# A recommender tower on one core: every burst's pair weights loaded as two tiles of 64 columns instead of one of 128

## What is computed

```python
e = jnp.stack([tbl_0[ids[:, 0]], ..., tbl_39[ids[:, 39]]], axis=1)      # 2048 x 40 x 32
vi = e[:, _I_IDX, :]; vj = e[:, _J_IDX, :]                              # 780 pairs
z = jnp.einsum('bke,kef,bkf->bk', vi, W, vj)
h = jnp.concatenate([z, dense_ctx], axis=1)
h = jnp.maximum(h @ W_top1 + b_top1, 0.0)                               # 796 -> 512
h = jnp.maximum(h @ W_top2 + b_top2, 0.0)                               # 512 -> 256
y = h @ W_top3                                                          # 256 -> 1
```

## Time and profile before

| | us |
|---|---|
| median of 3 runs | 719.52 |
| lowest and highest | 717.11, 720.22 |
| the profiled execution | 717.67 |
| span of its trace | 715.9 |
| PE busy in it | 661.3 |
| DVE busy | 548.0 |
| POOL busy | 441.1 |
| ACT busy | 67.3 |

### The profile page before, as it was taken

The page is one execution under the profiler, slowest core; times in us unless marked ns, Lnnn a source line. Parts: engine busy times, 40 slices in busy tenths (PEclk is TensorE's granted clock), DMA queues, the critical chain, the costliest instruction groups (busy, mean ns, idle before and its releaser), DMA issues.

```text
span 715.9 us, 13728 instructions
## 1 busy us (share of the span) xinstructions
PE 661.3 (92%) x5912; PEld 189.6 (26%) x5912; DVE 548.0 (77%) x518; ACT 67.3 (9%) x104; POOL 441.1 (62%) x452
## 2 busy tenths in 40 slices
PE   0769999997999999999889999999999999999998
PEld 0322232322222223232222222222222222222222
DVE  3858999987976679798777677979997677879900
ACT  4100000000001010001000110010001110010002
POOL 6777777777777777777777777777777730000000
PEclk9988999998999999999989999999999999999999
DMA  8761111033021111101322111011202200000000
GB/s 278 280 160 30 29 28 28 15 88 85 14 46 29 28 31 28 28 15 29 103 53 48 29 31 28 13 29 21 51 14 47 43 15 11 16 16 16 1 4 1
DMA packets 25124, 33.22 MB, mean 46 GB/s; under 512 B 10276, under 2 KB 18212, under 8 KB 24296
## 3 DMA queue, kind: packets, MB, share of 16 engines
q1 hardware_dynamic: 9720, 22.94, 10.6%
q0 software_dynamic: 14336, 7.37, 6.9%
q10 hardware_dynamic: 1008, 2.04, 0.8%
HBM read 21.77 MB, written 0.06 MB: 30 GB/s over the span
## 4 chain that ended last, share of the span: by engine, by line
PE 63%; DVE 12%; POOL 11%; issue 9%; DMA 3%; ACT 1%; DVEq 0%
PE t_ps L543 19%; PE z_ps L564 18%; POOL rows L364 11%; PE x_ps L583 11%; DVE prod L480 9%; PE t_ps L583 3%; PE x_ps L596 3%; DVE one_hot L458 3%; PE x_ps L505 3%; PE t_ps L551 2%; PE x_ps L521 2%; DMA hot_sb<-hot_ids 2%; PE x_ps L607 1%; PE t_ps L596 1%; ACT e_t L401 1%
## 5 line engine op out<-in xcount | busy, mean ns | idle before, releaser
L480 DVE TENSOR_TENSOR prod<-t_ps,e_t 128x1024 f32<-128x1024 f32 x400 | 467.9, 1218 | 99.6 <-PE t_ps L543 60.2
L364 POOL DMA_INDIRECT rows<-tbl,idx x448 | 440.9, 984 | 140.2 <-issue 135.9
L543 PE MATMUL t_ps<-e_t,w_sb 32*128 32x512 f32 x1440 | 223.4, 648 | 14.6 <-DVE prod L480 14.6
L564 PE MATMUL z_ps<-prod,select 128*32 128x512 f32 x1600 | 218.5, 604 | 2.0 <-DVE prod L480 1.3
L543 PEld LDWEIGHTS t_ps<-e_t,w_sb 32*128 32x128 f32 x1440 | 67.5, 185 | 169.9 <-DVE prod L480 89.1
L505 PE MATMUL x_ps<-one_hot,tables 128*32 128x512 bf16 x1272 | 85.8, 387 | 28.1 <-DVE one_hot L458 24.9
L458 DVE TENSOR_SCALAR one_hot<-hot_sb,row_number 128x2048 bf16<-128x2048 f16 (+1 forms) x112 | 79.7, 748 | 20.5 <-DMA hot_sb<-hot_ids 17.8
L583 PE MATMUL x_ps<-z_sb,w_sb 128*32 128x512 f32 x672 | 84.5, 601 | 0.0
L564 PEld LDWEIGHTS z_ps<-prod,select 128*32 128x32 f32 x1600 | 45.6, 110 | 102.9 <-issue 52.0
L505 PEld LDWEIGHTS x_ps<-one_hot,tables 128*32 128x32 bf16 x1272 | 29.5, 97 | 98.7 <-issue 41.5
L401 ACT COPY e_t<-x_ps 128x512 f32<-128x512 f32 x40 | 23.5, 587 | 270.5 <-PE x_ps L505 154.0
(11 more groups left out here) (18 smaller groups left out, 46.4 us busy)
## 6 DMA issues: line engine op xcount, KB each, us to landing
rows<-tbl,idx POOLq DMA_INDIRECT x448, 2.4
hot_sb<-hot_ids SPq DMA_DIRECT2D x4, 1536.0 KB, 7.3
e_t<-e_t SPq DMA_DIRECT2D x80, 64.0 KB
e_t<-e_t SPq DMA_DIRECT2D x40, 128.0 KB
w_sb<-w_lay SPq DMA_DIRECT2D x1, 1792.0 KB
z_sb<-hot_tables ACTq DMA_DIRECT2D x2, 640.0 KB, 6.3
w_sb<-w_lay SPq DMA_DIRECT2D x1, 1152.0 KB, 12.9
w_sb<-w_lay SPq DMA_DIRECT2D x1, 896.0 KB, 10.4
```

What stands on the lines that cost most here:

```text
L364: pool.indirect_dma_start(out=rows[:, slot, t, E * f:E * f + E], out_offset=None, in_=tables[PER * c + f], in_offset=bass.IndirectOffsetOn ...
L480: nc.vector.tensor_tensor(prod[:, u % PROD_SLOTS, :, :], t_ps[:, at:at + 2, :], by, ALU.mult).then_inc(mult_done, 1)
L543: mm = nc.tensor.matmul(t_ps[:, at + r % 2, :], w_sb[part, b, :], e_t[part, e_slot(k, g), :], start=True, stop=True)
L564: mm = nc.tensor.matmul(z_ps[E * q:E * q + E, :], select[:, E - PER - PER * s:2 * E - PER - PER * s], prod[:, u % PROD_SLOTS, q % 2, :], s ...
```

## The change

The two branches of `gen` become one: the bursts with g < c are written with the same inner loop over `side` as those inside a group. Each of their four matmuls with weights of 32x128 becomes two with weights of 32x64, which write partitions 0 to 63 and 64 to 127 of the same bank. Source rows, weights in SBUF, results, waits and semaphore counts stay as they were; the increment stays on the last matmul of r = 1 and of r = 3.

```diff
                     if g < c:
-                        mm = nc.tensor.matmul(t_ps[:, at + r % 2, :], w_sb[part, b, :], e_t[part, e_slot(k, g), :],
-                                              start=True, stop=True)
+                        near = far = e_slot(k, g)
                     else:
                         near, far = e_slot(k, c + r // 2), fold_slot(k, c + r // 2)
-                        for side in range(2):
-
-                            source = far if (r, side) in ((1, 0), (3, 1)) else near
-                            cols = slice(P // 2 * side, P // 2 * side + P // 2)
-                            mm = nc.tensor.matmul(t_ps[cols, at + r % 2, :], w_sb[part, b, cols], e_t[part, source, :],
-                                                  start=True, stop=True)
+                    for side in range(2):
+
+                        source = far if (r, side) in ((1, 0), (3, 1)) else near
+                        cols = slice(P // 2 * side, P // 2 * side + P // 2)
+                        mm = nc.tensor.matmul(t_ps[cols, at + r % 2, :], w_sb[part, b, cols], e_t[part, source, :],
+                                              start=True, stop=True)
```

## The result

| | before | after |
|---|---|---|
| median | 719.06 us (717.11 to 720.22, 5 runs) | 713.54 us (713.47 to 715.32, 5 runs) |
| ratio | | 0.9933, 95% interval 0.9912 to 0.9953 |
| profiled execution, its span | 717.67, 715.9 us | 713.47, 711.6 us |

The kernel got faster, by 4.8 us (0.67%) in this comparison. A closer one, with 8 runs of the changed kernel and 25 of the kernel before, gave less: 0.9966, interval 0.9954 to 0.9978, which is 2.4 us. The forecast was 2.6. On one other chip the same change cost 2.7 to 3.0%. Its ratio, put on the 719.5 us that the forecast started from, gives 714.7, and that of the closer one 717.1; both are inside. The forecast's own ratio, 0.9964, lies in the interval of the closer comparison and not in that of the first.

The account below looks back on a forecast made before the run. The chain was mostly TensorE (63%), with GpSimd's gathers setting the pace to 111.5 us and VectorE some later stretches. 95 chain bursts x 0.027 = 2.6 us, so 719.5 - 2.6 = 716.9 us; 8-in-10 range 713.8 to 720.5.

Parts of the forecast that it names:

- A burst costs 0.027 us less: Line 543's bursts: from first start to the next group 1.044 us with 64 columns, 1.071 with 128.
- an exposed load that goes by the columns less the spread of the starts: Inside a burst: shorter exposed weight load saves 0.054 us, later last starts give back 0.02 to 0.03.
- 95 bursts on the chain, 2.6 us: After 111.5 us: 95 of 160 line-543 bursts are tight pieces of the chain, each saving 0.027 us.
- the forecast's line of 0.5%: Whole kernel: 0.5%, 3.6 us, separates faster from no change; chances 0.27 faster, 0.67 within, 0.06 slower.
- The sign that the prediction named: First to last burst after 111.5 us: shrinking under 1.6 us means waited away, over 4 means more won.
- more is won than the chain shows: Rival: loops where VectorE and TensorE wait in turn get quicker, up to 4.3 us, 713.5 to 715.2 us; chance 0.14.
- what is saved ahead of the wait is waited: 0: About 20 longer chain bursts waiting for VectorE ahead of r = 2: claimed to gain 0.
- Up to 111.5 us the gathers set the pace, the early bursts bring 0: Chunk 0 up to group 7's transposes: 20 line-543 bursts only wait longer for the same gather, gain 0.
- The cover: Before 111.5 us: group 7's gathers hide the 20 early bursts, unless the gathers land earlier, which nothing here does.
- The slower rival, the instruction stream: Rival: 2880 more TensorE instructions, 10 more queue packets; late reading costs up to 24 us, 722 to 741 us; chance 0.05.
- The rules weighed against the trace: Skill's rules on bursts: same-row-group loads don't overlap, so no gain; per-matmul overhead, 32 us more; the trace disagrees with both.

Follow-up runs that it names:

- both close comparisons: Changed kernel against the kernel before, 714.33 to 717.03 us (0.9966); and 64 against 128 columns with the gathers left out of both, 714.73 to 717.16 us.
- after3: The changed kernel run again, against 25 runs of the kernel before: 714.33 us, ratio 0.9966.
- The two parts: 64 columns only in the 63 bursts of the first-dense-layer stretches (715.45 us, 0.9977), or only in the other 117 (715.40 us, 0.9978), each against the kernel before.
- early: 64 columns only in the 20 line-543 bursts ahead of group 7's transposes in chunk 0, against the kernel before: 717.42 us, ratio 0.9993.

## Why the prediction was right, and where it wasn't

- **A burst costs 0.027 us less.** Right: 1.04 on the chain, 0.48 to the second passes, 0.54 us for 20 bursts, in each of the traces with 64 columns, in the stretch of chunk 3. The working behind it, an exposed load that goes by the columns less the spread of the starts, held at 128 and 64. At 32 the load did as it said, but the starts cost more than the 7 ns counted on, from the fifteenth on.
- **95 bursts on the chain, 2.6 us.** Right in size: 2.4 us in both close comparisons, and 2.1 in the stages that repeat, with chunk 2's stretch not to be told. The first comparison had 4.8. Its interval and that of the close one miss each other by a hair (up to 0.9953, from 0.9954), and it leaves the forecast's 0.9964 out. By the forecast's line of 0.5% it was the outcome held for less likely (0.27), the close ones the likelier (0.67). It was of 5 and 5 runs, and about 2 of the 4.3 us between its two traces lie in places that vary without the change: the gathers' issues and two look-up stages. On which of these the rest of its runs gained isn't known. The sign that the prediction named, the time from the first to the last burst behind mark 0/7, says more than 2.6 too: 563.13 us before, 559.86 in the changed kernel's first trace, 558.86 in after3, and 559.73 and 556.49 for the two kernels without gathers. That is 3.3, 4.3 and 3.2 us less, once over its line of 4. What goes beyond the stages that repeat lies in stages that vary, and the medians of the close comparisons don't show it.
- **The rival "more is won than the chain shows"** (713.5 to 715.2 us) looked like the winner at first. The two parts and the close comparison speak against it, and so do single bursts. In the first pair the step from burst 43 to 44 in chunks 1 and 2 went from 3.580 to 3.457 us, which looks like a quicker loop between the engines. But with 128 columns it is 3.42 or 3.58: 3.424 and 3.420 in the kernel without gathers, 3.582 and 3.426 in "early", which has 128 there. Beside its quicker value 64 columns are 0.03 us slower. The rival had something all the same: the step that was too simple was "what is saved ahead of the wait is waited: 0". A wait at r = 2 splits a burst, and the half behind it has its own exposed load and fewer starts to give back, so it can save as well: in the last bursts of chunks 1 and 2, from the half's start to the next group, 1.058 us before and 1.018 after, by the starts in the two traces. It didn't add up to much, because VectorE sets most of these stretches: the stages from 1/7 to 1/9 and 2/7 to 2/9 gained 0.21 each.
- **Up to 111.5 us the gathers set the pace, the early bursts bring 0.** Right in the number (0.5, not told from 0), wrong in how firm it was. The cover is some 1.2 us in 68 (no-gather runs), and the text said that it wouldn't go.
- **The slower rival, the instruction stream.** At 0.05 it was held for unlikely. Where the kernel before takes 717 to 719 us it didn't happen: 11 more packets, no new idle time. On one chip it did, at 3%, through another door than the one described. The packets of the instruction queue were no slower there (about 1 us each in every trace), but TensorE started one instruction per 1.40 us in the worst stretch while gathers were issued, its signals came late, and what was added was worked off in GpSimd's pauses. The prediction's mechanism, a late packet, shows in no trace. That its 24 us for 2880 instructions came near the 31 to 35 measured is luck.
- **The rules weighed against the trace.** The Trainium skill's page "TensorE: Matmul & The Clock Gate", Part 3, has a weight load overlap matmuls in flight only if its row group is another one. Here sixteen loads of 131 ns, two to each row group and pass, take 0.23 us together, and four to each take 0.25 at 32 columns. The second load of a row group starts 7 ns after the first, with the row group's first matmul begun, so halves of a row group did overlap. The 60 cycles for each matmul of the Trainium skill's page "TensorEngine Tiling (Array Packing)", Instruction Overhead, don't show either: within a group a further start costs 7 ns, and 12 to 15 for the last two of sixteen.

## What to carry to other kernels

When the weight load ahead of a group of row-tiled matmuls is exposed, splitting its columns shortens the exposed part and adds starts; here that pays at 64 columns and not at 32. Count a small gain by the bursts on the chain, check it in stages that repeat to the hundredth, and don't trust a first pair of traces for the rest: 1 to 2 us of this kernel vary with no change, and a single step that looks won may have had both values before. A change that buys 0.4% with a quarter more TensorE instructions can cost 3% on a chip where they are slow to come, so time such a change on more than one chip.

## What the runs showed that I had not expected

- One chip ran the same program in 1174 us instead of 718, in all its runs of two series. In the worst stretches TensorE's starts stood 1.40 us apart with nothing that released them, between 30 and about 900 us, and a signal of it came 20 us late, while VectorE, ScalarE and GpSimd took their usual times for an instruction. While gathers were issued it got 6 instructions per us in each of three kernels; in GpSimd's pauses it caught up, and the last chunk ran at full pace. Added instructions cost 9 to 26 ns each in that part.
- Starts within a group of row- and column-tiled matmuls are 7 ns apart up to the fourteenth and 12 to 15 ns behind it (32 matmuls and 32 loads in a burst).
- Leaving out 448 gathers that held 11% of the chain gave 1 us, or some 4.5 us from mark 0/3 on, where the slower start of that run is left aside.
